# Cross attention of a decoder kernel: bf16 in three parts over 96 and 128 rows, or fp32r in two parts with one head per half of 64 rows

## The reference

```
x = x + xattn(layernorm(x), ctx, ctx)
# xattn(q, k, v): 32 query heads of width 16, 8 key/value heads of width 16;
# query heads 4g .. 4g+3 use key/value head g
scores = einsum('bkgsd,bktd->bkgst', q, k) / sqrt(16)
out    = einsum('bkgst,bktd->bkgsd', softmax(scores), v)
```

## Time and profile before

| | |
|---|---|
| median of 3 runs | 3719.46 us (3709.06 to 3720.39) |
| profiled execution, its own time | 3721.05 us |
| span of that execution in the trace | 3719.6 us |
| mean granted TensorE clock | 0.928 of full speed |
| cross attention stage in the trace | from 609.7 to 1189.6 us |
| of it before the first score matmul | to 664.0 us |

### The profile page before, as it was taken

How to read it: one execution, slowest core, us unless ns; L and a number is a source line. 1 busy time by engine, 2 the same in 40 slices (tenths; PEclk the granted TensorE clock), 3 DMA queues, 4 the chain that set the end, 5 groups by cost and what they waited for, 6 DMA issues and landing times.

```text
span 3719.6 us, 48990 instructions
## 1 busy us (share of the span) xinstructions
PE 3211.7 (86%) x18615; PEld 2165.4 (58%) x18615; DVE 2044.2 (55%) x3494; ACT 1552.5 (42%) x2639; POOL 1472.9 (40%) x1372
## 2 busy tenths in 40 slices
PE   7898885889898879999994799988999999448887
PEld 3343332333333448888883688877788888326654
DVE  2444443777876534444444445565545444568886
ACT  1222222577775324444441344433434444265443
POOL 2323323223221556666655434353433433114444
PEclk9899997899998799999997899999999999769998
DMA  3000000000001126566664101021010100210000
GB/s 109 1 1 1 1 1 9 4 1 1 1 1 60 42 69 194 196 195 194 194 195 128 48 24 45 29 77 34 27 41 23 42 27 7 102 46 9 12 12 15
DMA packets 134092, 206.49 MB, mean 56 GB/s; under 512 B 10810, under 2 KB 64911, under 8 KB 132708
## 3 DMA queue, kind: packets, MB, share of 16 engines
q1 hardware_dynamic: 116452, 152.98, 12.5%
q0 software_dynamic: 17408, 50.38, 4.7%
HBM read 161.29 MB, written 42.04 MB: 55 GB/s over the span
## 4 chain that ended last, share of the span: by engine, by line
PE 52%; DVE 18%; ACT 8%; issue 6%; POOL 2%; DMA 1%; another core or an unknown queue 0%; POOLq 0%; ACTq 0%; DVEq 0%; SPq 0%
PE ps L1412 9%; PE ps L1414 8%; PE ps L1413 8%; PE ps L2219 3%; PE ps L825 3%; PE ps L814 2%; PE ps L803 2%; DVE d_PTl L1936 2%; DVE d_mx L1921 2%; PE ps L1132 2%; DVE f_raw L2462 1%; PE ps L2240 1%; ACT d_PTh L1835 1%; ACT d_qk L1820 1%; DVE d_qk L1913 1%
## 5 line engine op out<-in xcount | busy, mean ns | idle before, releaser
L2029 POOL TENSOR_SCALAR d_P<-d_P,d_rv 128x128 f32<-128x128 f32 (+3 forms) x256 | 276.7, 1093 | 550.0 <-DVE d_rv L1929 549.8
L980 DVE TENSOR_REDUCE b_mx<-ps 128x2 f32<-128x1024 f32 x256 | 309.2, 1223 | 81.7 <-PE ps L803 74.7
L902 ACT ACTIVATE b_PT<-ps 128x512 f32<-128x512 f32 x512 | 291.5, 597 | 78.5 <-PE ps L814 68.6
L1534 POOL TENSOR_TENSOR x_wl<-x_wr,x_wh 128x1024 fp32r<-128x1024 f32 x96 | 227.4, 2392 | 184.6 <-ACT x_wh L1458 184.6
L1828 ACT ACTIVATE d_P<-ps,d_nb 128x128 f32<-128x128 f32 (+3 forms) x256 | 135.3, 529 | 259.0 <-DVE d_nb L1923 251.7
L814 PE MATMUL ps<-b_QT,b_KT 128*128 128x512 bf16 x512 | 196.8, 387 | 27.1 <-ACT b_PT L902 25.4
L1412 PE MATMUL ps<-d_xh,d_wh 128*128 128x512 f32 x512 | 214.2, 418 | 1.6 <-DVE d_xl L1898 1.6
L1936 DVE TENSOR_TENSOR d_PTl<-ps,d_PTh 128x384 fp32r<-128x384 f32 (+1 forms) x192 | 114.7, 598 | 166.2 <-ACT d_PTh L1835 166.2
L1413 PE MATMUL ps<-d_xl,d_wh 128*128 128x512 f32 x512 | 202.9, 396 | 0.0
L1414 PE MATMUL ps<-d_xh,d_wl 128*128 128x512 f32 x512 | 202.4, 395 | 0.0
L1412 PE MATMUL ps<-x_XH,x_wh 128*128 128x512 f32 x512 | 199.3, 389 | 1.4 <-DVE x_XL L1498 1.4
(11 more groups left out here) (359 smaller groups left out, 8846.3 us busy)
## 6 DMA issues: line engine op xcount, KB each, us to landing
x_wr<-in_L_ffn_w SPq DMA_DIRECT2D x32, 1024.0 KB
eoscr<-x_eo SPq DMA_DIRECT2D x32, 1024.0 KB, 5.5
x_wr<-in_L_ffn_w SPq DMA_DIRECT2D x32, 512.0 KB
d_w<-in_L_attn_W_Q SPq DMA_DIRECT2D x32, 256.0 KB
d_w<-in_L_attn_W_K SPq DMA_DIRECT2D x32, 256.0 KB
d_w<-in_L_attn_W_V SPq DMA_DIRECT2D x32, 256.0 KB
d_wo<-in_L_attn_W_O SPq DMA_DIRECT2D x16, 512.0 KB, 3.8
X<-in_x SPq DMA_DIRECT2D x4, 1024.0 KB, 13.5
```

Of the source, the lines that this page charges most:

```text
L902: e.activation(M.PT[:, half, y, h, :], ps[:, 4 + y, :], ACT.Exp, scale=0.25).then_inc(S["b_ex"], 1)
L980: e.tensor_reduce(M.mx[:, r % 2, c0:c0 + 2], ps[:, 2 * (t % 2):2 * (t % 2) + 2, :], AX.X, ALU.max).then_inc(S["b_mx"], 1)
L1534: e.tensor_tensor(M.wl[:, z, k:k + 2, :], W.wr[:, z, k:k + 2, :], M.wh[:, z, k:k + 2, :].bitcast(F32), ALU.subtract).then_inc(S["x_wl"], 1)
L2029: e.tensor_scalar(P, P, M.rv[:, y, q:q + 1], None, ALU.mult).then_inc(S["d_nm"], 1)
```

## The change: what it does, and the diff

- Stacks are f32 tiles with 64 columns per head: high part, low part, high part again (16 columns each), two columns for the maximum in two parts, 14 zeros. The parts are fp32r. `b_QG` holds the four heads of one group for all 512 rows, three groups in turn; POOL fills it per group (`gather`) from the norms, which are kept for the whole batch (`b_xn`).
- A spare use turns two heads at once: 4 f32 transposes of 128x128 with the two heads' 64 columns side by side, so that one head lies on rows 0 to 63 and the next on rows 64 to 127. `one` turns the stack without maxima for the scores (`b_Q1`), `two` turns the same stack again after POOL has put in the maxima (`b_Q2`). Both are copied out by ACT (128x512).
- The spare uses of a group are `one` at steps 1 and 5, `two` at steps 2 and 6, `settle` at step 3, and in groups g = 2 to 5 of batches 0 to 2 the keys at steps 0 and 4 (4 f32 transposes each; copied out by ACT for batch 0, by DVE for the others). Turns of whole tiles and `rows` are gone.
- `scores` and `exps` contract over 64 rows in fp32r. One step of `scores` holds the two heads of a pair (rows 0 to 63, then 64 to 127) for one tile of queries; both go to different banks. The `exps` matmuls of a step are both of one head, so on one half.
- Key stacks are made by DVE for batch 0 and by POOL for the others (`cross_keys`, 3 instructions a tile). The norms of batches 1 to 3 are made by POOL. The statistics of the next batch move from group 2 to group 1 on DVE.

```diff
     def step(self, n, s):
         if n < 0:
-            return [("keys", 0, t) for t in range(4)] + [("turn", 0, t, g) for t in range(4) for g in range(4)] if s == 0 else []
+            return [("keys", 0, t, h) for t in range(4) for h in range(2)] + [("one", 0)] if s == 0 else []
...
-            if b + 1 < B and s in (0, 1, 4, 5):
-                i = s // 4 * 2 + s % 2
-                if g == 2:
-                    out.append(("keys", b + 1, i))
-                if g >= 4:
-                    out.append(("turn", b + 1, g - 4, i))
+            if b + 1 < B and 2 <= g <= 5 and s in (0, 4):
+                out.append(("keys", b + 1, g - 2, s // 4))
+            if s == 1:
+                out.append(("one", 2 * n + 1))
+            if s == 5 and n + 1 < self.N:
+                out.append(("one", 2 * n + 2))
+            if s == 6:
+                out.append(("two", 2 * n))
         if s == 2 and 1 <= n <= self.N:
-            out.append(("rows", 2 * n - 1))
-        if s == 6 and n < self.N:
-            out.append(("rows", 2 * n))
+            out.append(("two", 2 * n - 1))
...
+    M.QG = sb("b_QG", [128, 3, 4, 4, 64])
+    M.Q1, M.Q2 = sb("b_Q1", [128, 4, 512], FR), sb("b_Q2", [128, 4, 512], FR)
...
+def cross_keys(e, S, own, M, b, t_i):
...
+    e.tensor_copy(M.KS[:, y, :, :, 16:32].bitcast(FR), s4)
+    t = own.inc(e.tensor_copy(M.KS[:, y, :, :, 0:16].bitcast(FR), s4))
+    e.wait_ge(own.sem, t)
+    e.tensor_tensor(M.KS[:, y, :, :, 32:48], s4, M.KS[:, y, :, :, 0:16], ALU.subtract).then_inc(S["b_KS"], 1)
...
+            for q in range(4):
+                t = e.transpose(bank[:, q * 128:q * 128 + 128], M.QG[:, n % 3, q, 2 * p:2 * p + 2, :].rearrange("p a d -> p (a d)"), G.ident)
...
-            i = e.matmul(ps[:, 2 * (t % 2) + y, :], M.QT[b % 2][0:96, 4 * g + s // 2, q * 128:q * 128 + 128], M.KT[0:96, b % 2, g, :], start=True, stop=True)
+        for h in range(2):
+            rows = slice(64 * h, 64 * h + 64)
+            i = e.matmul(ps[:, 2 * (t % 2) + h, :], M.Q1[rows, r % 4, q * 128:q * 128 + 128], M.KT[rows, b % 2, g, :], start=True, stop=True)
...
+        rows = slice(64 * (h % 2), 64 * (h % 2) + 64)
...
-        e.matmul(ps[:, 4 + y, :], M.KT[:, b % 2, g, k * 128:k * 128 + 128], M.QT[b % 2][:, 4 * g + h, :], start=True, stop=True).then_inc(S["b_exp"], 1)
+        e.matmul(ps[:, 4 + y, :], M.KT[rows, b % 2, g, k * 128:k * 128 + 128], M.Q2[rows, (2 * j + h // 2) % 4, :], start=True, stop=True).then_inc(S["b_exp"], 1)
...
+    def gather(n):
...
+        t = po.inc(e.tensor_copy(part[:, :, :, 0:16].bitcast(FR), src))
+        if n >= 3:
+            e.memset(part[:, :, :, 48:50], 0.0)
+        e.wait_ge(po.sem, t)
+        e.tensor_tensor(part[:, :, :, 16:32], src, part[:, :, :, 0:16], ALU.subtract)
+        e.tensor_copy(part[:, :, :, 32:48], part[:, :, :, 0:16]).then_inc(S["b_QG"], 1)
```

More of the change, by code:

```diff
@@ L766, in spare @@
         if kind == "keys":
-            b, t_i = use[1:]
+            b, t_i, h = use[1:]
             e.wait_ge(S["b_KS"], 4 * b + t_i + 1)
-            for g in range(8):
-                t = e.transpose(pv[:, g * 128:g * 128 + 128], M.KS[:, t_i % 2, g, :, :].rearrange("p a d -> p (a d)"), G.identb)
+            for y in range(4):
+                t = e.transpose(bank[:, y * 128:y * 128 + 128], M.KS[:, t_i % 2, 4 * h + y, :, :].rearrange("p a d -> p (a d)"), G.ident)
             t.then_inc(S["b_KSp"], 1)
[L772 to L786, removed]
+        elif kind in ("one", "two"):
+            r = use[1]
+            n, p = divmod(r, 2)
+            if kind == "one":
+                e.wait_ge(S["b_QG"], n + 1)
+            else:
+                e.wait_ge(S["b_parts"], r + 1)
+            for q in range(4):
+                t = e.transpose(bank[:, q * 128:q * 128 + 128], M.QG[:, n % 3, q, 2 * p:2 * p + 2, :].rearrange("p a d -> p (a d)"), G.ident)
+            t.then_inc(S["b_onep" if kind == "one" else "b_twop"], 1)
         else:
@@ L846, in cross_act @@
     ps, O = G.ps, CROSS
[L847 to L858, removed]
+    bank = ps[:, 6, :]
@@ L877, in cross_act @@
[L877 to L886, removed]
+        if kind == "keys" and use[1] == 0:
+            t_i, h = use[2:]
+            e.wait_ge(S["b_KSp"], 2 * t_i + h + 1)
+            e.activation(M.KT[:, 0, 4 * h:4 * h + 4, t_i * 128:t_i * 128 + 128], four(bank), ACT.Copy).then_inc(S["b_spare"], 1)
+        elif kind == "one":
+            r = use[1]
+            e.wait_ge(S["b_onep"], r + 1)
+            if r >= 4:
+                e.wait_ge(S["b_sc"], 4 * r - 12)
+            e.activation(M.Q1[:, r % 4, :], bank, ACT.Copy).then_inc(S["b_spare"], 1)
+        elif kind == "two":
+            r = use[1]
+            e.wait_ge(S["b_twop"], r + 1)
+            if r >= 4:
+                e.wait_ge(S["b_exp"], 16 * (r // 2 - 1))
+            e.activation(M.Q2[:, r % 4, :], bank, ACT.Copy).then_inc(S["b_spare"], 1)
@@ L887, in cross_act @@
+    for use in O.at[-1, 0]:
+        spare(use)
     for n in range(O.N + 4):
         for s in range(8):
[L889 to L892, removed]
             for use in O.at[n, s]:
@@ L906, in cross_dve @@
     ps, O, dv = G.ps, CROSS, Own(S["dve"])
[L907 to L938, removed]
     ln_stats_dve(e, S, dv, G, range(4))
     for t_i in range(4):
-        keys(0, t_i)
+        cross_keys(e, S, dv, M, 0, t_i)
+    e.wait_ge(S["ln_rstd"], 1)
     for t_i in range(4):
[L944 to L949, removed]
+        ln_apply(e, G, t_i, M.xn[:, 0, t_i, :]).then_inc(S["b_xn"], 1)
     for n in range(O.N + 4):
@@ L993, in cross_pool @@
     O, po = CROSS, Own(S["pool"])
[L994 to L996 removed]
+    e.memset(M.KS[:, :, :, :, 48:64], 0.0)
+    t = po.inc(e.memset(M.V[:, :, :, :, 16:32], 0.0))
     e.wait_ge(po.sem, t)
[L998 to L1003 removed]
+    e.memset(M.KS[:, :, :, :, 48:50], 1.0).then_inc(S["b_init"], 1)
@@ L1038, in cross_pool @@
     ln_rstd_pool(e, S, G, range(4), 1)
     for t_i in range(4):
-        keys(0, t_i)
-        split(t_i)
+        values(0, t_i)
+    gather(0)
     for n in range(O.N + 4):
@@ L1044, in cross_pool @@
             b, g = O.work[n]
-            if b + 1 < B and 3 <= g < 7:
-                split(4 * b + 4 + g - 3)
+            if n + 1 < O.N:
+                gather(n + 1)
             parts(2 * n)
-            if b + 1 < B and g == 2:
-                for t_i in range(4):
-                    keys(b + 1, t_i)
-                ln_rstd_pool(e, S, G, range(4 * b + 4, 4 * b + 8), b + 2)
+            if b + 1 < B:
+                if g == 2:
+                    ln_rstd_pool(e, S, G, range(4 * b + 4, 4 * b + 8), b + 2)
+                    e.wait_ge(S["ln_rstd"], b + 2)
+                if 1 <= g <= 4:
+                    cross_keys(e, S, po, M, b + 1, g - 1)
+                    values(b + 1, g - 1)
+                if 2 <= g <= 5:
+                    ln_apply(e, G, 4 * b + 4 + g - 2, M.xn[:, (b + 1) % 2, g - 2, :]).then_inc(S["b_xn"], 1)
             parts(2 * n + 1)
```

124 lines of the change are left out of this document (48 added, 76 removed).

## The result

The changed kernel takes **3666.9 us** (median of 4 runs, 3661.01 to 3672.62) against 3717.91 us before (4 runs, 3709.06 to 3720.39): ratio 0.986, 95% interval 0.983 to 0.989. It is 51 us faster. The forecast was 73 us; the measured time lies inside its range, 20 us above its point. The profiled execution took 3666.91 us itself, its span is 3665.5 us.

What follows compares the result with a forecast made beforehand. A group was taken as an in-order path on PE with ACT's releases in it. Gains of 34.4 us before the first score and 38.4 over three batches, 72.8 together, gave a median of 3647 us, range 3615 to 3697.

Steps and rivals of the forecast that it cites:

- Prologue, 34.4: Before the first score: nine uses of the bank at 1.73 us, first score at 629.6 instead of 664.0, gain 34.4 us.
- Halves run at once: In each step, a score on one row half runs beside work on the other: three slots, 0.68 us, not four.
- Rival 1: Halves do not run at once: four slots, 0.91 us a step, quiet group 15.4, preparing 17.2, total 3687 us; chance 0.15.
- rival 2: Weight loads on the same half not hidden: three of 0.19 us a step, total 3753 us, slower; chance 0.08.
- exps 0.45 apart: Sign inside a step: the second exps matmul stands 0.45 us behind the first, the two scores starting together.
- Change of shape 0.10, four turns 0.47: PE prices in a group: each change of the array's shape about 0.10 us, four f32 transposes 0.47 us.
- Rival 3: Changes of shape cost nothing: 13.5 us a group, 19 us more gain, total 3628 us; chance 0.12.
- Quiet group 14.1: Group preparing nothing for the next batch: step pairs 2 x 3.13 + 2 x 3.92 = 14.1 us, against 14.06 before.
- preparing 16.0: Group also turning keys for the next batch: two uses cost 1.87 us together, so 16.0 us, against 17.36 before.
- First batch 12.8: Each of the first three batches: 4 x 14.1 + 4 x 16.0 = 120.4 us against 133.2, gain 12.8 us.
- clock held low longer: Example case under "anything else", beside POOL running late; chance 0.05 for all of these.
- rival 4: ACT becomes the bound: an exponential 0.3 us late at steps 2 and 6 gives 3666; shares the forecast's chance, 0.60.

Runs made afterwards that it cites:

- the first experiment: Against the changed kernel, all score and exps matmuls use rows 0 to 63, the odd heads' products left out: 3722.4 us.
- the two kernels with DVE's copies: On top of the crossing, DVE instead of ACT copies every `two` out of PSUM, or only that of step 6: 3659.4 and 3653.33 us.
- the crossing: Against the changed kernel, a step's two exps are of both heads of a pair, one per half, and scores take the halves in reverse order: 3650.59 us.
- the kernel with added matmuls: Against the changed kernel, unread bf16 128x512 matmuls on bank 7 from the stage's start to the first values: 3658.36 us.
- the kernel over 128 rows: Against the changed kernel, scores and exps contract over all 128 rows, summing the two heads of a pair: 3671.68 us.
- the three crossed ones with added matmuls: The crossing plus unread bf16 matmuls on bank 7: 3630.87 us; then `two` from step 6 to 7: 3625.23; then second keys from step 4 to 6: 3613.67.
- the last two kernels of this document: On the crossing plus unread bf16 matmuls: `two` moved from step 6 to 7, 3625.23 us; then also second keys from step 4 to 6, 3613.67 us.

## Why the prediction was right in sign, and 20 us off

- **Prologue, 34.4: right** (33.9). A keys use took 1.80 us for the 1.73 forecast, the first score came 20.4 us into the stage. One use in full, beside the earlier trace rows:

```profile
614.54 1.11 PE L786 MATMUL ps<-cst,b_KS 128*128 128x128 f32 x4 [0.69 <-ACT b_KT L868]
615.69 0.60 ACT L868 ACTIVATE b_KT<-ps 128x512 fp32r<-128x512 f32 x1 [1.20 <-PE ps L786]
616.34 1.11 PE L786 MATMUL ps<-cst,b_KS 128*128 128x128 f32 x4 [0.69 <-ACT b_KT L868]
```

- **Halves run at once: right.** The timeline shows common starts, and taking them away costs 1.61 us a group. Rival 1 as I priced it gave 15.4 a group and 3687; it would have been 16.04 and no gain at all. It was a larger risk than the prediction made of it: its four slots and the change of shape behind them take 1.12 us, where it had 0.91 + 0.10.
- **Loads on one half hidden: right but for the first.** By my own sign for rival 2 (gaps of 0.3 or more on one half without a wait) there is one such gap a step, 0.34, and the second is 0.23. The prediction had the 0.34 in its price list and applied it after waits only. That is the **step that failed**: "exps 0.45 apart" was 0.57, 0.12 in every step; the 0.11 belongs to every first fp32r matmul behind f32 work, wait or not. The weight loads show what differs: the first exps' load starts together with its matmul (1026.51 and 1026.52), the second's 0.23 ahead of it (1026.86 and 1027.09):

```profile
1026.51 0.18 PEld L829 LDWEIGHTS ps<-b_Q,b_KT 64*128 64x128 f32 x1 [0.84 <-issue]
...
1026.86 0.18 PEld L829 LDWEIGHTS ps<-b_Q,b_KT 64*128 64x128 f32 x1
```

  The rule of the Trainium skill ("TensorE: Matmul & The Clock Gate", Part 3), that a load overlaps a running matmul only for another row group, would make every slot on one half long; the 0.23 slots of the first experiment, all on one half, speak against it as a rule for this stream.
- **Change of shape 0.10, four turns 0.47**: out 0.09, right; the turns with the return 0.58, where 0.57 was the sum. The sum is luck in part: with no change of shape the turns take 0.35 to 0.42 up to the next exps, so the return costs about 0.2. Rival 3 (13.5 a group) is out: shapes cost 1.16 us.
- **Quiet group 14.1: measured 14.43; preparing 16.0: measured 16.4.** The added 0.12 a step makes 0.25 in the pairs (4, 5) and (0, 1) (3.38 and 3.36 for 3.13). The other two pairs came near their 3.92 by another path than forecast. I had both end on ACT's second exponential at 2.40. But neighbours on ACT start 0.49 apart and not 0.58 to 0.60, as they overlap; the 2.33 / 4 of the earlier trace rows held waits for PE:

```profile
1034.17 1.08 ACT L895 ACTIVATE b_PT<-ps 128x512 f32<-128x512 f32 x2 [0.82 <-PE ps L829]
```

  So in the pair 2 and 3 PE waits for nothing, and its own slots and turns make the 3.95; in the pair 6 and 7 it waits 0.29 for the first exponential, and the pair ends at 3.75. The waits for `b_PT` at steps 2 and 6 that I named as a sign are one wait a group, at step 7. The cost of these groups is 4 x 0.33 + 4 x 0.4 = 2.9 of the 3.7 us that each batch missed, and in the last batch, where I had put 0, a group went from 14.06 to 14.43: 8 x 0.37 = 3.0 of its 3.7.
- **DVE's statistics, put at nothing: 0.7 a batch.** I wrote that they cost again what they cost now; but the 133.2 of before holds that cost, and my 120.4 has no term for it. In two batches a turn of `one` waits for DVE's copy of the keys, which stands behind the statistics of the next batch (2.46 us at 767.29):

```profile
773.28 0.65 PE L796 MATMUL ps<-cst,b_QG 128*128 128x128 f32 x4 [0.72 <-DVE b_KT L918]
```

- **The wait for settle's division before the keys: right**, 0.72 for 0.73, eleven times in the waits of PE:

```profile
PE ps L786 <- DVE b_tmp L941: 7.9, 11, 0.7
```

- **First batch 12.8: wrong, 1.5.** Beside the 3.7 of every batch and 3.2 in the first groups, the clock: 4.4 us, which stood only as "clock held low longer" within a chance of 0.05. I took the full clock for granted behind the first score, since before it came 17 us behind its own. It came 34 us behind.
- **ACT the bound (rival 4): no.** Its 10.57 of 14.43 us busy and the two kernels with DVE's copies show that its load is not it; what PE waits for it is 0.29 us a group, in the loop of step 7. That this rival's 3666 is the measured time is a coincidence: it had an exponential 0.3 late at steps 2 and 6, and no such wait is there.
- **POOL: nothing, right.** It is busy 3.46 us in a quiet group and 8.27 in a preparing one, and no wait on it stands among PE's. Its norm took 2.09 us, where 1.5 was forecast; hidden all the same. For DVE the nothing was wrong, as said.

The forecast of 3647 was 20 us low: the stage's misses, 0.5 + 11.3 + 7.5 + 3.7 = 23, less 1.2 by which the medians differ by more than the stages (51.0 and 49.8) and 1.5 by which the kernel before measured lower this time (3717.91 for 3719.46).

## What to carry to other kernels

When matmuls on two halves of the array run at once, a step costs what the fuller half costs: count slots per half, and alternate both kinds of work over them. Put the turns of a shared bank where the chain PE, ACT, PE leaves PE without work, and not where PE is the bound; the crossing, two such moves and the clock's 8 us were worth as much again as the whole change. An engine that looks busy isn't at full clock for that: read the granted clock behind the change as a row of its own. And when single executions are compared, look first at the stretch that the edit doesn't touch: here it moved the stage by 2 us between two kernels with the same code before the first score.

## What the runs showed of the hardware that was not expected

- 64-row fp32r work, with f32 turns of 128 rows between, kept PE busy for 12.98 of 13.00 us at a granted 0.50 (1.2 GHz). The clock rose to 1.00 at 654.1, 4.3 us behind the first values, f32 over 128 rows:

```profile
649.79 1.93 PE L840 MATMUL ps<-b_PT,b_V 128*32 128x512 f32 x8
```

  In every kernel with 64-row scores and no added matmuls it rose 1.3 to 4.3 us behind the first values. The same schedule over 128 rows rose at 624.9, 23 us ahead of its values. Holding the clock is another matter: once at 1.00, it stayed there through 8.7 us of 64-row work with the turns (634.0 to 642.7 in the kernel with added matmuls), and in the change through every later group. It fell there, in the kernel over 128 rows and in the three crossed ones with added matmuls, at the end of the same gap in PE's work, 1.4 to 1.7 us of waiting for the maxima, or up to 2.3 us behind it; in the last two kernels of this document added matmuls over 128 rows were still to come. That the gap is the reason was not tried.
- The first fp32r matmul behind f32 turns or values occupies 0.34 us instead of 0.23, on 64 and on 128 rows.
- Of the two scores of a step, the one on the half that the first exps leaves free starts with it, the other 0.34 later. In the step at 1026.52 the individual records show the later-issued score (the one that signals `b_sc`) starting first and ending at 1027.02, the earlier-issued one ending at 1027.24 (both ends are modelled). The semaphore rose only at 1027.27, and DVE, which waits for it, began behind that:

```profile
1027.29 1.23 DVE L932 TENSOR_REDUCE b_mx<-ps 128x2 f32<-128x1024 f32 x1
```

  So it is in 121 of the stage's 256 pairs: the start is out of the order of issue, the signal isn't.
